# Twelve of 32 heads by the dense route, with quads ordered by three tables and dense tiles alternating between two banks

## The chip, the cores and the metric

One core of one Trainium2 chip runs the whole program. The metric is the device time in microseconds of one execution. The engines named below are PE (TensorE, matmul), PEld (its weight loads), DVE (VectorE), ACT (ScalarE), POOL (GpSimd) and SP (SyncE).

## The reference, cut to what matters

The program is a four-block tower over a stream `h` of 4 x 2048 tokens of 64 values. The change touches only the last stage, the feed-forward of block 3, which is attention whose keys and values come from a table, picked by product keys:

```python
def _pk(x, Wq_pk, pk_keys):                       # 8 heads, 64 keys a side
    q = (x @ Wq_pk).reshape(b, n, 2, 8, 32).transpose(2, 0, 1, 3, 4)
    sim = jnp.einsum('pbnhd,pkhd->pbnhk', q, pk_keys)
    scores, idx = jax.lax.top_k(sim, 16)
    index = idx[0][..., :, None] + 64 * idx[1][..., None, :]
    score = scores[0][..., :, None] + scores[1][..., None, :]
    final_scores, pk_idx = jax.lax.top_k(score.reshape(..., 256), 16)
    return softmax(final_scores), take_along_axis(index.reshape(..., 256), pk_idx)
q = (x @ Wq).reshape(b, n, 8, 64) * 64 ** -0.5
kv_scores, ind = _pk(x, Wq_pk, pk_keys)            # ind + head * 4096
k = einsum('bnhk,bnhkd->bnhd', kv_scores, keys_table[ind])
v = einsum('bnhk,bnhkd->bnhd', kv_scores, values_table[ind])
sim = einsum('bihd,bjhd->bhij', q, k)              # 2048 x 2048, causal
out = softmax(causal(sim)) @ v ; h = h + out.reshape(b, n, 512) @ Wo
```

So each (batch, head), 32 in all, needs for each token a weighted sum of 16 table rows, and then causal attention over 2048 tokens.

## The kernel before, in words

`mix_heads` does this stage. Work is cut into *quads*: 512 tokens (four tiles of 128) of one (batch, head). There are 128 quads, four to a head, and the attention tile at depth i (0 to 15) of a head looks at i+1 blocks of keys, that is at i // 4 + 1 chunks of 512.

A quad gets its mixed table rows in one of two ways. **Gathered** (6 of 8 heads of each batch, 96 quads): DVE picks the 16 rows (`top`, `top_pairs`) and turns them to row numbers (`decode`); POOL issues 16 indirect DMAs for each tile of 128 tokens, a *unit* (L2239); ACT scales each of the 16 landed rows (*copies*, `part_up`, L2430); DVE adds them up (`sum_up`, L2656). **Dense** (2 of 8 heads, 32 quads): DVE picks and ranks (`rank`, `centre`); no gather is made. Instead the whole table of the head is walked in 32 *pieces* of 128 rows. A piece is `level` (one bf16 matmul of 512 columns to the bank `DX`, L2318), `lift` (ACT, L2469), `cross` (four bf16 matmuls to the same bank, L2324 and L2325), `grow` (ACT exp, L2473) and `blend` (an f32 matmul, in two passes, that adds to `acc`, L2334). `store` (DVE, L2686) ends the quad.

All engines run through one list of *steps*, 16 to a row of 34 rows, each in its own program order. A step holds, where it exists: one attention tile n (`scores` of tile n+1 L2291, `attend` on ACT L2456, `flip` L2298, `take_flip` L2465 and `mixing` L2308 for each chunk; `peak` L2667 and `scale` L2677 on DVE), two pieces (16 steps x 2 = the 32 pieces of one dense quad), the picks of one tile of a later quad, and in three of four steps one unit of 16 copies. In every fourth step `make` turns a quad's key, value and query for attention. `scores` of tile n+1 writes the same PSUM tile `S` (four banks) that the exp of tile n reads, so it waits for that exp (`expd`); the exp of tile n+1 waits for the last mixing of tile n (`mixed`), for `peak` of tile n+1, and for whatever ACT's program has ahead of it. With one bank for pieces, `level` of a piece waits for `grow` of the one before.

POOL may run GOT = 4 units ahead of ACT's copies.

Of the kernel before, what the change touches and what calls it, by code (L numbers as in the profile page):

```python
# [13 lines left out]
ALU = mybir.AluOpType  # L14
# [1955 lines left out]
DENSE = 2  # L1970
GATHER = HEADS - DENSE
QUAD = 4
ROWS = B * DENSE * TPB // QUAD
GOT, RING = 4, 5
TILES = KEYS * KEYS // P
# [99 lines left out]
def picks(r):

    order = ("g0", "d", "g1", "g2") if r < 0 else ("d", "g0", "g1", "g2")
    return [("d", r + 1) if k == "d" else ("g", 3 * (r + 1) + int(k[1])) for k in order]


def attended(r, q):

    if r < 0 or r > ROWS:
        return None
    kind, g = (("g", 3 * r - 2), ("g", 3 * r - 1), ("d", r - 1), ("g", 3 * r))[q // QUAD]
    if g < 0 or g >= (ROWS if kind == "d" else 3 * ROWS):
        return None
    return kind, g


def mix_heads(nc, table, h, hT, ident, ones, wsim, iota, wq, wo, mask, lanes, sel, counts, push, least):

    wsim_h = wsim[:].rearrange("d (p h k) -> d h p k", p=2, h=HEADS)
    tiles = [(r, q) for r in range(0, ROWS + 1) for q in range(16) if attended(r, q)]
    number = {rq: n for n, rq in enumerate(tiles)}
    depth = [QUAD * (attended(*rq)[1] % QUAD) + rq[1] % QUAD for rq in tiles]
# [21 lines left out]
    def pieces(r, q):

        return [TILES * r + 2 * q + i for i in range(2)] if 0 <= r < ROWS else []  # L2120

    def dense_at(r):

        return 4 * [k for k, _ in picks(r)].index("d")

    def pick_before(r, q, by):

        r, q = following(r, q, -by)
        return (r, q // QUAD) if -1 <= r < ROWS - 1 else None

    def pick_after(r, q):

        r, q = following(r, q)
        return (r, q // QUAD) if q % QUAD == 0 and r < ROWS - 1 else None

    def made_at(r, q):

        ahead = number.get(following(r, q, 2))
        nxt = number.get(following(r, q))
        if q % QUAD == 2 and ahead is not None and not late(*attended(*tiles[ahead])):  # L2140
            return ahead
        if nxt is not None and nxt % QUAD == 0 and late(*attended(*tiles[nxt])):
            return nxt
        return None
# [730 lines left out]
```

## Time and profile before

| what | us |
|---|---|
| median of 3 runs | 14013.33 (14011.51 to 14019.07) |
| the profiled execution | 14017.65 |
| its span, first to last instruction | 14015.6 |
| mean granted TensorE clock over the span | 0.768 |
| busy in the span: PE, DVE, ACT, POOL | 9358.8, 9539.3, 6297.5, 7987.4 |
| first and last start of a gather (L2239) | 5841.5, 13773.4 |

Times of rows count from the start of the span. PE durations overlap (a matmul's end is modelled), so the mean of one row is longer than the pitch at which such matmuls follow each other. A row of idle time names the instruction that ended it.

### The profile page before, as it was taken

The page shows a single profiled execution, that of the slowest core. Times are in us where ns is not written, and L with a number is a line of the kernel's source. Part 1 is how long each engine was busy: PE and PEld are TensorE (multiplying, and loading weights), DVE is VectorE, ACT ScalarE, POOL GpSimd, SP SyncE. Part 2 cuts the span into 40 slices and gives each one's busy share as a digit, 9 for nine tenths or more (in the row PEclk, how much of TensorE's full clock was granted, in tenths as well). Part 3 has the DMA queues.
Part 4 walks back from the last instruction along what each step waited for, and adds up shares of the span by engine and source line. Part 5 has one row for each costly group of instructions (what it writes and reads, how often), then busy time and mean ns, then how long its engine had stood idle before and what let it go on. Part 6 is the DMA issues. An engine that isn't in the chain of part 4 may idle for free.

```text
span 14015.6 us, 129357 instructions
## 1 busy us (share of the span) xinstructions
PE 9358.8 (67%) x34236; PEld 4949.2 (35%) x34236; DVE 9539.3 (68%) x21923; ACT 6297.5 (45%) x13845; POOL 7987.4 (57%) x6892
## 2 busy tenths in 40 slices
PE   1556455455545655277887877877877877877777
PEld 0343122122213122134444434444444444444444
DVE  3332988888883874777777676677777677776751
ACT  0111333334321012156666666666666666666653
POOL 3000566666650000277777777777777777777772
PEclk9655777777775776578887888878888888888886
DMA  1000222222220000111222212212222112112220
GB/s 25 1 14 3 92 102 97 97 98 97 103 90 10 12 8 6 29 51 52 58 52 53 56 51 55 55 51 56 53 52 57 52 52 57 52 51 58 52 52 23
DMA packets 305053, 730.88 MB, mean 52 GB/s; under 512 B 130242, under 2 KB 170737, under 8 KB 269914
## 3 DMA queue, kind: packets, MB, share of 16 engines
q0 software_dynamic: 201216, 405.72, 11.1%
q1 hardware_dynamic: 103178, 317.81, 6.7%
q8 instruction: 239, 3.92, 0.1%
q14 instruction: 420, 3.44, 0.1%
HBM read 706.25 MB, written 8.42 MB: 51 GB/s over the span
## 4 chain that ended last, share of the span: by engine, by line
POOL 38%; issue 12%; PE 5%; DVE 2%; ACT 1%; DVEq 0%; DMA 0%; POOLq 0%; ACTq 0%
POOL l3m_got L2239 38%; PE l3m_O L2308 1%; PE l3m_S L2291 1%; PE l3m_T L2298 1%; PE l3m_acc L2334 1%; PE l3m_DX L2324 0%; ACT l3m_spread L2430 0%; ACT l3m_probT L2465 0%; ACT l3m_prob L2456 0%; PE l3m_T L2278 0%; DVE l3m_hot L2596 0%; DVEq L2592 0%; PE l3m_T L2265 0%; DVE l3m_hot L2593 0%; DVE l3m_hot L2589 0%
## 5 line engine op out<-in xcount | busy, mean ns | idle before, releaser
L2239 POOL DMA_INDIRECT l3m_got<-in_l_table,l3m_row x6144 | 6036.4, 982 | 1938.9 <-issue 1868.7
L2430 ACT ACTIVATE l3m_spread<-l3m_got,l3m_weight 128x128 f32<-128x128 f32 x6136 | 2109.6, 490 | 437.8 <-DMA l3m_got<-in_l_table,l3m_row 432.5
L2334 PE MATMUL l3m_acc<-l3m_W,l3m_values 128*128 128x512 f32 x2048 | 1343.8, 744 | 142.8 <-ACT l3m_W L2473 138.4
L1262 POOL TENSOR_TENSOR m_mul<-m_st,m_wide_c 128x2048 f32<-128x2048 f32 x256 | 1157.4, 4521 | 150.0 <-DVE m_st L1415 143.8
L2308 PE MATMUL l3m_O<-l3m_vo_g,l3m_probT 128*128 128x64 f32 x6528 | 1003.9, 299 | 317.7 <-ACT l3m_probT L2465 306.3
L2308 PEld LDWEIGHTS l3m_O<-l3m_vo_g,l3m_probT 128*128 128x128 f32 x6528 | 950.8, 215 | 723.7 <-ACT l3m_probT L2465 643.0
L2465 ACT ACTIVATE l3m_probT<-l3m_T 128x512 f32<-128x512 f32 (+3 forms) x1280 | 692.9, 541 | 1005.9 <-PE l3m_T L2298 1003.9
L2291 PE MATMUL l3m_S<-l3m_kvT_g,l3m_qT 64*128 64x512 f32 (+3 forms) x1920 | 751.2, 755 | 575.0 <-ACT l3m_prob L2456 561.4
L1295 PE MATMUL m_W<-m_mul,tower_ident 128*128 128x512 f32 (+1 forms) x1536 | 836.9, 667 | 206.9 <-POOL m_mul L1262 205.9
L2677 DVE SCALAR_TENSOR_TENSOR tower_h<-l3m_O,l3m_pinv,tower_h 128x64 f32<-128x64 f32 x512 | 145.4, 284 | 1195.1 <-PE l3m_O L2308 1173.6
L2469 ACT ACTIVATE l3m_V<-l3m_DX,l3k_least 128x512 bf16<-128x512 f32 x1024 | 699.5, 683 | 429.7 <-PE l3m_DX L2318 421.5
L2656 DVE TENSOR_REDUCE l3m_kv<-l3m_spread 128x128 f32<-128x2048 f32 x384 | 871.9, 2271 | 20.4 <-ACT l3m_spread L2430 20.4
L1308 PE MATMUL m_W<-m_split,l1a_sel 128*128 128x512 bf16 x1024 | 374.4, 455 | 764.6 <-DVE m_st L1415 752.7
L2298 PE MATMUL l3m_T<-tower_ident,l3m_prob 128*128 128x128 f32 x4352 | 843.1, 317 | 34.0 <-ACT l3m_prob L2456 34.0
L2473 ACT ACTIVATE l3m_W<-l3m_DX 128x512 f32<-128x512 f32 x1024 | 608.1, 594 | 409.4 <-PE l3m_DX L2325 404.6
L2298 PEld LDWEIGHTS l3m_T<-tower_ident,l3m_prob 128*128 128x128 f32 x4352 | 589.4, 172 | 452.2 <-issue 398.7
L2456 ACT ACTIVATE l3m_prob<-l3m_S,l3m_nmax 128x128 f32<-128x128 f32 (+15 forms) x512 | 589.8, 1152 | 292.8 <-DVE l3m_nmax L2667 272.7
L2667 DVE TENSOR_REDUCE l3m_nmax<-l3m_S 128x1 f32<-128x128 f32 (+15 forms) x512 | 661.2, 1291 | 40.3 <-issue 1.1
L1405 DVE TENSOR_TENSOR m_W<-m_dtx,m_W 128x1024 f32<-128x1024 f32 x512 | 618.5, 1208 | 22.0 <-PE m_W L1308 21.4
L2291 PEld LDWEIGHTS l3m_S<-l3m_kvT_g,l3m_qT 64*128 64x128 f32 x1920 | 253.5, 246 | 1032.3 <-ACT l3m_prob L2456 824.3
L1415 DVE TENSOR_TENSOR_SCAN m_st<-m_dA,m_st,m_W 128x1024 f32<-128x1024 f32 x256 | 600.8, 2347 | 22.0 <-issue 2.7
L1415 DVE TENSOR_TENSOR_SCAN m_st<-m_dA,m_W 128x1024 f32<-128x1024 f32 x256 | 585.5, 2287 | 41.3 <-POOL m_mul L1262 7.2
(677 smaller groups left out, 18538.4 us busy)
## 6 DMA issues: line engine op xcount, KB each, us to landing
m_wide_c<-l1a_c SPq DMA_DIRECT2D x256, 1024.0 KB, 4.7
l3m_got<-in_l_table,l3m_row POOLq DMA_INDIRECT x6144
l3m_values<-in_l_table SPq DMA_DIRECT2D x32, 512.0 KB, 3.9
l0i_img<-in_l_x SPq DMA_DIRECT2D x4, 1024.0 KB, 8.0
l2r_x<-l2a_hT SPq DMA_DIRECT2D x8, 512.0 KB, 5.5
qp_inw<-in_q_inw SPq DMA_DIRECT2D x1, 2336.0 KB, 7.8
l_kept<-l0t_xt,l0t_row POOLq DMA_INDIRECT x128, 2.2
l1a_c<-m_mul SPq DMA_DIRECT2D x16, 128.0 KB, 2.6
```

What stands on the lines that cost most here:

```text
L1262: pool.tensor_tensor(mul[:, k % 2], st[:, k % 2], wide_c[:, k % CRING], ALU.mult).then_inc(multiplied, 1)
L1295: last = pe.matmul(W[:, 1, lo:hi], ident[:], mul[:, k % 2, lo:hi], start=(k == 0), stop=(k == 2 * DS - 1))
L1415: dve.tensor_tensor_scan(st[:, k % 2, half(hf, k)], dA[:, k % 2, half(hf, k)], W[:, 0, half(hf, k)], first, ALU.mult, ALU.add).then_inc(sw ...
L2239: pool.indirect_dma_start(got[:, unit % GOT, j, :], None, table, bass.IndirectOffsetOnAxis(ap=row[:, unit // QUAD % RING, unit % QUAD, j:j ...
L2291: last = pe.matmul(S[:, c * CH:hi], qT[k:k + D, slot, t * P:(t + 1) * P], kvT[kind][k:k + D, c * CH:hi], start=True, stop=True)
L2298: last = pe.transpose(T[:, (a % 4) * P:(a % 4 + 1) * P], prob[:, a * P:(a + 1) * P], ident[:])
L2308: last = pe.matmul(O[:, n % 2 * D:(n % 2 + 1) * D], probT[:, (chunk0[n] + c) % 2, (a % 4) * P:(a % 4 + 1) * P], vo[kind][:, a, :], start=( ...
L2334: pe.matmul(acc[:], values[:, tile, :], W[:], start=(tile == 0), stop=(tile == TILES - 1)).then_inc(blended, 1)
L2430: last = act.activation(spread[:, unit % 2, :, j], got[:, unit % GOT, j, :], ACT.Copy, scale=weight[:, g % RING, t, j:j + 1])
L2465: act.activation(probT[:, k % 2, 0:to], T[:, 0:to], ACT.Copy).then_inc(t_taken, 1)
L2469: act.activation(V[:], DX[:], ACT.Relu, bias=least[:], scale=-1.0).then_inc(lifted, 1)
L2656: dve.tensor_reduce(out[:, ::-1, :] if g % 2 else out, spread[:, unit % 2].rearrange("p (s d) j -> p s d j", s=2), AX, ALU.add).then_inc(s ...
```

## The change

Five of the eight heads of each batch are gathered and three are dense: 20 heads (80 quads, 5120 gathers) and 12 heads (48 quads, 1536 pieces). The rows of 16 steps give way to one list of 537 steps, with three tables: the order in which quads are picked (`pick_order`), the order in which they are attended (`attend_order`), and the rates of pieces and copies. From step 9 each step has three pieces (`first_piece`), from step 13 each has ten copies (`copies`), a unit may begin and end inside a step, and tiles begin at step 24. A unit is added up by DVE in the step after its last copy.

About every second piece uses the fourth bank of `S` where neither tile n nor n+1 needs it (depth under 12, `wide`): 565 of the 1536. Where a piece and the one before it use different banks (`other`), `level` comes ahead of the earlier piece's `blend`, and waits only for the `grow` two pieces back. `scores` of a tile at depth 12 or more also waits for `grow` of the last piece that used that bank. `make` is always in the third step of a quad, and `scores` of the next tile is no longer held behind it.

```diff
-DENSE = 2
-GATHER = HEADS - DENSE
+GATHERED = (5, 5, 5, 5)
+PERIOD, BEFORE = 20, (0, 2, 4, 5, 8, 9, 10, 12, 14, 16, 18, 19)
+LAG, UNITS_FROM, PIECES_FROM = 6, 12, 9
+DQ, GQ = QUAD * len(D_HEADS), QUAD * len(G_HEADS)
+QUADS = DQ + GQ
+STEPS = QUAD * (QUADS + LAG) + 1
+COPIES = TOPK * GQ // QUADS
+def first_piece(s):
+    return TILES * DQ * (s - PIECES_FROM) // (QUAD * QUADS)
+def pick_order():
+    def due(kind, i):
+        if kind == "g":
+            return UNITS_FROM + QUAD * TOPK * i / COPIES - 6
+        return PIECES_FROM + QUAD * QUADS * i / DQ - 9
+    return sorted([("g", i) for i in range(GQ)] + [("d", i) for i in range(DQ)], key=lambda x: (due(*x), x[0]))
+def attend_order():
+    order, d = [], 0
+    for g in range(GQ):
+        if g % PERIOD in BEFORE:
+            order.append(("d", d))
+            d += 1
+        order.append(("g", g))
+    return order
...
+    second, spare = set(), False
+    for s in range(STEPS):
+        for k in pieces(s):
+            spare = not spare and not wide(s)
+            if spare:
+                second.add(k)
...
+                if i >= 3 * QUAD and behind:
+                    pe.wait_ge(grown, behind)
...
             def level(k):
                 if k % TILES == 0:
                     pe.wait_ge(taild, k // TILES + 1)
                 if k:
-                    pe.wait_ge(grown, k)
-                pe.matmul(DX[:], sel[:, k % TILES, :], ranksT[:, k // TILES % 2, :],
+                    pe.wait_ge(grown, k - 1 if other(k) else k)
+                pe.matmul(bank(k), sel[:, k % TILES, :], ranksT[:, k // TILES % 2, :],
                           start=True, stop=True).then_inc(levelled, 1)
...
             def onward(k):
+                if other(k):
+                    level(k)
                 if k >= 1:
                     blend(k - 1)
-                level(k)
+                if not other(k):
+                    level(k)
...
+                for c in range(max(chunks, len(todo))):
+                    if c < chunks:
+                        flip(n, c)
+                    if c < len(todo):
+                        cross(todo[c])
+                    if c < chunks:
+                        mixing(n, c)
+                    if c + 1 < len(todo):
+                        onward(todo[c + 1])
+                if made_at(s):
+                    make(*made_at(s))
...
+                part_up(mine[0:share])
+                chunks = depth[n] // 4 + 1 if n is not None else 0
+                for c in range(max(chunks, len(todo))):
+                    if c < chunks:
                         take_flip(n, c)
+                    if c < len(todo):
+                        grow(todo[c])
+                    part_up(mine[(c + 1) * share:(c + 2) * share])
+                    if c + 1 < len(todo):
+                        lift(todo[c + 1])
+                part_up(mine[(max(chunks, len(todo)) + 1) * share:])
```

## Rows read from the trace of the kernel before

**Rows 1.** The page: the gather, its count, busy time, mean ns, idle.
```profile
L2239 POOL DMA_INDIRECT l3m_got<-in_l_table,l3m_row x6144 | 6036.4, 982 | 1938.9 <-issue 1868.7
```
**Rows 2.** Waits from 5841 to 13773: who for whom, us in total, times, longest.
```profile
POOL l3m_got L2239 <- issue: 1868.4, 6131, 0.3
...
ACT l3m_spread L2430 <- DMA l3m_got<-in_l_table,l3m_row: 432.5, 98, 10.5
...
DVE l3m_tail L2708 <- ACT l3m_mid L2488: 163.4, 31, 10.7
...
POOL l3m_got L2239 <- DVE l3m_row L2626: 42.5, 1, 42.5
...
POOL l3m_got L2239 <- ACT l3m_spread L2430: 27.7, 11, 24.1
```
**Rows 3.** Stretches: length, busy us of PE, PEld, DVE, ACT, POOL; clock, DMA, GB/s.
```profile
8000.00:10000.00 2000.00, 1583.30 (x6542) 877.93 (x6541) 1415.77 (x4545) 1239.29 (x3111) 1526.42 (x1555) 0.82 0.21 54
13773.00:14016.00 243.00, 171.69 (x617) 115.98 (x614) 36.13 (x53) 53.55 (x87) 1.04 (x2) 0.56 0.04 10
```
**Rows 4.** The same view, eight quads: depths 0-3, 4-7, 8-11, 12-15, two of each.
```profile
8060.27:8110.11 49.84, 41.69 (x118) 18.00 (x116) 37.74 (x137) 31.61 (x89) 37.65 (x41) 0.70 0.20 53
8350.12:8408.39 58.27, 43.79 (x121) 18.86 (x119) 50.65 (x153) 32.27 (x88) 45.55 (x42) 0.69 0.18 47
8110.11:8170.54 60.43, 43.25 (x177) 22.48 (x177) 53.19 (x153) 35.82 (x93) 47.02 (x45) 0.83 0.19 49
8476.72:8535.99 59.27, 47.29 (x173) 26.55 (x171) 40.89 (x146) 35.53 (x93) 44.95 (x48) 0.80 0.20 54
8170.54:8231.08 60.54, 49.07 (x236) 29.34 (x236) 41.66 (x139) 43.04 (x106) 45.91 (x49) 0.89 0.20 52
7850.84:7916.86 66.02, 52.07 (x231) 29.25 (x232) 55.03 (x154) 39.75 (x97) 51.70 (x48) 0.82 0.21 57
7992.18:8060.27 68.09, 57.07 (x278) 35.30 (x277) 40.89 (x129) 43.31 (x102) 51.63 (x55) 0.92 0.20 53
8596.90:8665.97 69.07, 53.63 (x279) 32.57 (x278) 55.32 (x153) 43.66 (x101) 53.70 (x51) 0.88 0.18 49
```
**Rows 5.** PE by line, 5780 to 14016: busy us, mean ns, idle before.
```profile
L2334 PE MATMUL l3m_acc<-l3m_W,l3m_values 128*128 128x512 f32 x2048 | 1343.8, 744 | 142.8 <-ACT l3m_W L2473 138.4
...
L2324 PE MATMUL l3m_DX<-l3m_high,l3k_sel 128*128 128x512 bf16 x1024 | 460.1, 449 | 175.6 <-ACT l3m_V L2469 175.0
```
**Rows 6.** Timeline of PE inside one deep tile: start us, us, what.
```profile
9008.59 0.61 PE L2298 MATMUL l3m_T<-tower_ident,l3m_prob 128*128 128x128 f32 x4
9009.04 1.02 PE L2334 MATMUL l3m_acc<-l3m_W,l3m_values 128*128 128x512 f32 x2
9009.90 0.38 PE L2318 MATMUL l3m_DX<-l3m_ranksT,l3k_sel 128*128 128x512 bf16 x1
9010.13 1.11 PE L2308 MATMUL l3m_O<-l3m_vo_d,l3m_probT 128*128 128x64 f32 x8
```
**Rows 7.** Timeline of ACT, the same tile.
```profile
9015.58 1.82 ACT L2456 ACTIVATE l3m_prob<-l3m_S,l3m_nmax 128x1920 f32<-128x1920 f32 x1
...
9017.97 1.38 ACT L2430 ACTIVATE l3m_spread<-l3m_got,l3m_weight 128x128 f32<-128x128 f32 x4
```
**Rows 8.** Stretches in the head: DVE picks a gathered quad, then a dense one.
```profile
5812.33:5841.30 28.97, 4.15 (x16) 3.56 (x16) 26.05 (x116) 3.63 (x11) 0.00 (x0) 0.50 0.23 60
5841.30:5885.10 43.80, 0.33 (x2) 0.33 (x3) 38.84 (x134) 0.27 (x2) 33.83 (x33) 0.50 0.19 48
```
**Rows 9.** DVE by line, 6000 to 13700: the sum of a unit.
```profile
L2656 DVE TENSOR_REDUCE l3m_kv<-l3m_spread 128x128 f32<-128x2048 f32 x377 | 856.0, 2271 | 13.6 <-ACT l3m_spread L2430 13.6
```
**Rows 10.** First and last start of two lines: similarities, then the exp of attention.
```profile
L2257 PEld LDWEIGHTS l3m_T<-l3k_wsim,l3f_hT x1024: 182/330/336, 5809.6 to 13469.5; 64*128 64x128 f32 x171
...
L2456 ACT ACTIVATE l3m_prob<-l3m_S,l3m_nmax x512: 361/1161/1967, 6072.4 to 13982.2; 128x896 f32<-128x896 f32 x12, 128x1280 f32<-128x1280 f32 x12, 128x128 f32<-128x128 f32 x11, 128x512 f32<-128x512 f32 x11
```

More of the change, by code:

```diff
@@ L2118, in pieces @@
[L2118 to L2144, printed above, removed]
@@ new lines, in copies, with unit_summed, dense_picked, made_at @@
+    def copies(s):
+        j = COPIES * (s - UNITS_FROM - 1)
+        return range(max(j, 0), max(min(j + COPIES, QUAD * TOPK * GQ), 0))
+    def unit_summed(s):
+        ends = [j // TOPK for j in copies(s - 1) if j % TOPK == TOPK - 1]
+        return ends[0] if ends else None
+    def dense_picked(s, by):
+        p, t = pick_at(s - by)
+        return picks[p][1] if t == 0 and picks[p][0] == "d" else None
+    def made_at(s):
+        n = tile_at(s + 2)
+        return kinds[n] if n is not None and n % QUAD == 0 else None
@@ L2280, in make, with scores @@
                 last.then_inc(t_made, 1)
[L2282 to L2283 removed]
+            def scores(n, behind):
+                kind, g = kinds[n]
                 i, slot = depth[n], n // QUAD % 2
@@ L2363, in _ @@
                 if todo:
                     onward(todo[0])
-                elif r == ROWS and q == 0:
-                    blend(TILES * ROWS - 1)
-                made = made_at(r, q)
-                held = made is not None and made == nxt
-                if nxt is not None and not held:
-                    scores(nxt)
+                elif pieces(s - 1):
+                    blend(TILES * DQ - 1)
+                if nxt is not None:
+                    scores(nxt, max((k + 1 for k in second if k < first_piece(s)), default=0))
@@ L2684, in store @@
                     dve.wait_ge(placed, g)
-                dve.wait_ge(t_taken, T_at["inverse", g - 1] + 1)
+                dve.wait_ge(t_taken, T_at["inverse", g] + 1)
                 dve.tensor_tensor(stage[:], acc[:], invT[:, g % 2, :], ALU.mult).then_inc(staged, 1)
-            for r, q in steps:
-                n = number.get((r, q))
+            for s in range(STEPS):
+                n = tile_at(s)
+                todo = pieces(s)
+                done = [(i, k // TILES - 1) for i, k in enumerate(todo) if k and k % TILES == 0]
+                if not todo and pieces(s - 1):
+                    done = [(0, DQ - 1)]
+                when, held = done[0] if done else (None, None)
```

377 lines of the change are left out of this document (170 added, 207 removed).

## The prediction, made before the change was run

> **What bounds the kernel now.** I read first who never rests. POOL issues 6144 gathers in the stage, each 0.982 us long with 0.304 us of issue time behind it (1868.7 us over 6144), 1.286 us together [rows 1]. Times 6144 that is 7901 us, and the gathers run from 5841.5 to 13773.4, which is 7932 us. POOL waited for anything else for only 42.5 + 27.7 us [rows 2]. So POOL is the bound of this stage, and the first question is what stands right behind it.
>
> Next I read how late POOL's work really is to the others. The copies on ACT waited for landed rows 98 times, 432.5 us in all [rows 2]. Over 128 quads of attention that is 3.4 us a quad. This is the number on which everything hangs: the others wait for POOL for 5% of the stage, so without POOL they are at most 5% quicker by themselves.
>
> Third, the other engines in the steady stretch. In 2000 us PE is busy 1583, DVE 1416 and ACT 1239, at a granted clock of 0.82 [rows 3]. None is full. They wait for each other in turn: scores wait for the exp, the exp for mixing, mixing for ACT's copy of the flipped tile. I call that the ring. A step is 1/4 quad; POOL's bound gives 12 units x 16 x 1.291 us / 16 = 15.5 us a step (1.291 is 7932 over 6144).
>
> Fourth, what one turn of the ring costs by depth. The pairs of [rows 4] give 54.1, 59.9, 63.3 and 68.6 us a quad for one to four chunks, mean 61.5. The clock is 0.70 for the shallowest and 0.90 for the deepest quads, where PE is busy 83.8% and 77.6% of the time against 83.6% and 75.2%: PE's time in shallow quads is bought at half clock. For all 128 quads I take the first exp at 6072.4 [rows 10] to the end at 14015.6: 7943.2 us, 62.06 us a quad, which holds the tail too (243 us after the last gather, at a clock of 0.56 [rows 3]).
>
> **The change, part by part.** All terms are for one quad (four steps) unless said.
>
> *Gathers.* 1024 fewer: POOL needs 5120 x 1.291 = 6610 us, 51.6 us a quad where the ring takes over 58. It leaves the bound, and the 3.4 us go: 62.06 - 3.38 = 58.68. What is late next is the ring.
>
> *Pieces.* Three a step for two, so four more a quad. On PE at full clock a piece is a blend, 0.86 us from its start to the next matmul (9009.04 to 9009.90), and five bf16 passes at 0.23 (9009.90 to 9010.13), 2.0 us in all [rows 6]. By the mean durations of the stage it is 1.49 + 5 x 0.449 = 3.7 us [rows 5], but these overlap; scaled by 0.82, the clock of the stretch, 2.0 becomes 2.45. On ACT it adds a lift and a grow beside that. Bounds for four: 0, if they fall into time in which PE now waits (417 of 2000 us, 12.9 us a quad [rows 3]), and 4 x 2.95 = 11.8 if each is paid with its waits for `lift` (175.6 us over 1024 pieces) and `grow` (142.8 over 1024) as well [rows 5]. I split by depth. In deep quads a chunk's time on PE is all work: flip, cross, mixing, then blend and level; 4 x 2.0 is paid nearly whole, 8 us for four chunks and 7 for three. In shallow quads DVE is the longer partner: it is busy 50.65 of 58.27 us and 53.19 of 60.43 when it picks a dense quad, plus drains [rows 4]. There the third piece runs beside DVE, and the second bank takes a blend out of the way of each lift (1128 of 1535 changes of piece). I take 2 and 4 us. The mean is 5.2.
>
> *Copies.* 40 for 48 a quad. Four take 1.38 us [rows 7], one some 0.30 after another, so -2.4 on ACT. They also move: before, four copies stood last in a step, right ahead of the next exp; now that place holds one or none. But the fourth step of a quad, which had none, now has ten. Bounds -2.4 and 0; I take -1.9.
>
> *Picks and sums on DVE.* Picking a dense quad takes 43.8 us, a gathered one 29.0 plus four sums of 2.27, 38.1 [rows 8, 9]. 16 quads change sides: 16 x 5.7 = 91 us, 0.7 a quad if DVE set every step, 0 if none. There are also 16 more turns of the dense ranks (ACT's `mid`, for which DVE waited 163.4 us in 31 quads [rows 2]), up to 84 us or 0.7. I take 0.6 for both.
>
> *A wait that is new.* The scaled rows lie in two buffers, so unit u's first copy waits until unit u-2 is added up. Before, that was two steps back. Now a unit is 1.6 steps long and is added in the step after its last copy; for u = 3, 8, 13 and so on (64 of 320) the first copy falls in the same step, behind the ninth copy, in which DVE adds unit u-2 after its picks. DVE gets there some 9 to 12 us into the step (a quad's picks of 29.0 or 43.8 over four tiles, then 2.27), ACT at 7 to 12. Queued behind the waiting copy are the lift of the third piece and so PE's cross and the next exp. 64 waits of 0 to 4 us are 0 to 2.0 us a quad; I take 0.6.
>
> *Second bank, tables, held scores.* `level` ahead of `blend` is in the piece term. A deep tile's new wait for `grown` is for pieces of earlier steps, which are long done: nothing. Un-holding `scores` behind `make` (24 quads) gives under 1 us each: nothing taken. SP's table loads rise from 32 to 48 and have a head's 32 pieces of lead: hidden, as SP's loads are not among the waits.
>
> *Head and tail.* From the first similarity to the first exp it is 262.8 us [rows 10]. Now six quads are picked there, three of each kind: 3 x 43.8 + 3 x 29.0 = 218 [rows 8], with pieces from step 9 and copies from step 13 beside them. 218 to 263; I take 240, so the first exp is at 6050. At the end 16 tiles run without pieces where 12 did, all of the two deep kinds: +12 us.
>
> **The sum.** 5.2 - 1.9 + 0.6 + 0.6 = +4.5 us a quad on 58.68: 63.2. 6050 + 128 x 63.2 + 12 = 14,150. The profiled execution (14017.65, span 14015.6) is 4 us above the median of the runs, so no correction is due. Forecast: 14,150 us, +1.0%. The gain from POOL (-433 us) and the dearer ring (+576) nearly cancel, and small errors of one piece's price decide the sign: 1 us a quad is 128 us, and the break-even is at +3.4 us a quad.
>
> **The rivals.**
>
> *The clock comes back (faster).* PE works 12.26 us a step at a clock of 0.82 [rows 3], which is 10.05 us at full clock. With a third piece it is 12.05. If the denser array holds a mean clock of 0.92, as the deep quad at 7992 had it [rows 4], PE is busy 13.1 us a step, 0.8 more than now, and with the idle time that POOL does not cause (3.23 - 0.84 = 2.4) a step is 15.5; at 0.96 it is 14.95. The mean, 15.2, gives 60.8 us a quad, and with head and tail as above and 50 us for the last quads at half clock, 6050 + 7784 + 50 = 13,880. For it: the clock in [rows 4] rises with the share of work. Against it: the ring still has the exp's gap in each step (1.82 us of exp with 1.1 of PE work beside it [rows 7, 6]), and it is such gaps after which the clock is low. Chance 0.36 for this side, from -0.2% down to 13,500.
>
> The Trainium skill (TensorE: Matmul & The Clock Gate, "What's actually happening") says that the throttled clock is the default state and that activity releases it. The rows agree (0.56 in the tail, 0.92 in a deep quad); taken as strongly as it is put there it speaks for this rival.
>
> *POOL stays the bound.* If the ring had slack that the 432.5 us do not show, the gathers set the end: the first about 44 us later (a dense quad is picked first [rows 8]), 5885 + 6610 + 243 = 12,740. Against: the deepest quads already take 68 to 69 us while POOL's share is 62, so they are ring-bound now. Chance 0.03.
>
> *Each piece is paid in full (clearly slower).* With 2.95 us a piece in every step the term is 11.8 for 5.2: 14,150 + 6.6 x 128 = 14,995. The place is `cross` waiting for `lift` and `grow` waiting for `cross`, three times a step, with copies between; it decides above 0.85 us a piece (3.4 / 4). For: in a one-chunk tile there is little attention work to lay beside three pieces. Against: DVE's load hides it there. Chance of over 14,600: 0.10; it ends at the slower side like the forecast.
>
> *Nothing moves,* within 0.2% (28 us, about what a measurement of this kernel can tell from no change): the break-even by chance, 0.09.
>
> **How the numbers follow.** Forecast and its neighbourhood, 14,040 to 14,600: 0.42. Faster 0.39 (0.36 + 0.03), same 0.09, slower 0.52. With the piece term between 2 and 8.5 us the time is 13,740 to 14,570; I reach down to 13,550 for the clock and up to 14,600. The likeliest case alone: 14,040 to 14,400.
>
> **What would show it right or wrong.** Gathers with idle time between them that ends on `spread` (ACT) or on `row` (DVE), not on issue alone; the wait of `spread` for DMA gone (under 50 us) and a new one of `spread` for `kv` (DVE), some 80 us; the granted clock in the steady stretch at 0.84 to 0.88; PE busy 86 to 90% of it; quads of one chunk near 52 us, quads of four chunks near 73. A clock of 0.92 or more, or deep quads under 70 us, would make the rival right. If copies still wait for DMA by hundreds of microseconds, the first reading was wrong.

## The result, and the profile after

| what | before | after |
|---|---|---|
| median of 4 runs, us | 14012.42 (14010.05 to 14019.07) | 14271.05 (14258.20 to 14284.90) |
| profiled execution, us; its span | 14017.65; 14015.6 | 14258.20; 14256.5 |
| mean granted clock over the span | 0.768 | 0.813 |
| gathers, first and last start | 6144, 5841.5 to 13773.4 | 5120, 5887.3 to 13961.2 |
| first exp of attention [rows 10] | 6072.4 | 6058.1 |

The ratio is 1.0183, with the interval 1.0171 to 1.0196: the change costs 259 us. Forecast was +1.0%, 14,150. The sign and the range (13,550 to 14,600) held the result; the size did not come out: +138 was expected and +259 came. So two questions are left: is the first reading true (POOL is the bound, and gives 433 us back when it is relieved), and which term of the dearer ring was too small?

Shares of the whole span by the chain that ended last, from the page of after. Before, POOL had 38% of it and issue 12%, PE 5%.

```profile
PE 36%; ACT 11%; DVE 5%; issue 4%; DVEq 2%; POOL 1%; ACTq 0%; DMA 0%; POOLq 0%
```

The gather and the copy, from the page of after: count, busy us, mean ns, then idle us before them and what ended it. The first answers [rows 1].

```profile
L2258 POOL DMA_INDIRECT l3m_got<-in_l_table,l3m_row x5120 | 5065.2, 989 | 3096.4 <-issue 1516.9
L2449 ACT ACTIVATE l3m_spread<-l3m_got,l3m_weight 128x128 f32<-128x128 f32 x5120 | 1926.9, 495 | 43.0 <-issue 36.7
```

A gather costs what it cost (989 ns for 982), but 3096.4 us lie idle before them where 1938.9 did, and only 1516.9 of that is issue. What ended the rest stands in the waits of after from 5841 to 13900 (who for whom, us, times, longest), which answer [rows 2]:

```profile
POOL l3m_got L2258 <- issue: 1501.6, 4880, 1.5
...
POOL l3m_got L2258 <- ACT l3m_spread L2449: 1050.8, 165, 26.7
...
ACT l3m_W L2492 <- PE l3m_DX L2352: 678.9, 961, 2.8
...
POOL l3m_got L2258 <- DVE l3m_row L2642: 528.7, 25, 86.7
...
PE l3m_S L2312 <- ACT l3m_prob L2475: 418.6, 331, 5.0
...
DVE l3m_stage L2700 <- PE l3m_acc L2361: 300.5, 46, 14.4
...
ACT l3m_spread L2449 <- DMA l3m_got<-in_l_table,l3m_row: 6.3, 2, 5.7
```

POOL now waits for the others (1050.8 and 528.7 us), and the copies' wait for landed rows fell from 432.5 us to 6.3. No wait of `spread` for `kv` is among them.

Stretches of after, which answer [rows 3] and [rows 4]: length, busy us of PE, PEld, DVE, ACT and POOL, clock, DMA, GB/s. The third is a quad of one chunk, the fourth a quad of four, the last the tail.

```profile
8000.00:10000.00 2000.00, 1704.45 (x7258) 923.68 (x7256) 1400.27 (x4481) 1296.54 (x3051) 1226.53 (x1241) 0.90 0.17 45
...
8319.60:8382.66 63.06, 56.07 (x258) 32.38 (x257) 50.25 (x135) 42.16 (x97) 37.96 (x38) 0.89 0.17 43
8870.59:8925.15 54.56, 42.24 (x145) 17.73 (x144) 48.46 (x156) 33.44 (x89) 39.05 (x37) 0.91 0.16 44
8382.66:8461.99 79.33, 67.74 (x325) 40.65 (x324) 45.05 (x148) 50.79 (x111) 33.78 (x36) 0.89 0.15 41
14000.00:14256.00 256.00, 180.22 (x634) 123.18 (x634) 35.63 (x52) 59.41 (x102) 0.00 (x0) 0.54 0.04 9
```

(The second row is a quad of three chunks.) PE is busy 85% of the steady stretch where it was 79%, and the clock rose from 0.82 to 0.90. Over all quads of one chunk it went from 0.72 to 0.90. And still they are not shorter (54.8 us before, 55.1 after).

### The profile page after: what moved, and what is told of

It is laid out like the page before. It is cut to its first block, busy times and chain, and to the rows that moved or that the text cites. A ratio compares the mean times of both kernels' runs of the same rounds, so it can differ in the third digit from the quotient of the medians.

```text
span 14256.5 us, 136705 instructions
## 1 busy us (share of the span) xinstructions
PE 10105.4 (71%) x38012; PEld 5286.1 (37%) x38012; DVE 9606.4 (67%) x22115; ACT 6689.9 (47%) x13997; POOL 7015.6 (49%) x5868
## 4 chain that ended last, share of the span: by engine, by line
PE 36%; ACT 11%; DVE 5%; issue 4%; DVEq 2%; POOL 1%; ACTq 0%; DMA 0%; POOLq 0%
PE l3m_S L2312 7%; PE l3m_O L2329 6%; PE l3m_acc L2361 5%; PE l3m_DX L2351 5%; PE l3m_T L2319 3%; ACT l3m_spread L2449 2%; PE l3m_S L2351 2%; ACT l3m_prob L2475 2%; ACT l3m_V L2488 2%; PE l3m_T L2276 2%; PE l3m_DX L2352 1%; ACT l3m_W L2492 1%; PE l3m_T L2297 1%; POOL l3m_got L2258 1%; PE l3m_DX L2345 1%
## 5 line engine op out<-in xcount | busy, mean ns | idle before, releaser
L2258 POOL DMA_INDIRECT l3m_got<-in_l_table,l3m_row x5120 | 5065.2, 989 | 3096.4 <-issue 1516.9
L2449 ACT ACTIVATE l3m_spread<-l3m_got,l3m_weight 128x128 f32<-128x128 f32 x5120 | 1926.9, 495 | 43.0 <-issue 36.7
L2361 PE MATMUL l3m_acc<-l3m_W,l3m_values 128*128 128x512 f32 x3072 | 1791.6, 667 | 186.4 <-ACT l3m_W L2492 180.5
L2329 PEld LDWEIGHTS l3m_O<-l3m_vo_g,l3m_probT 128*128 128x128 f32 x5440 | 760.9, 206 | 251.9 <-ACT l3m_probT L2484 179.3
L2329 PE MATMUL l3m_O<-l3m_vo_g,l3m_probT 128*128 128x64 f32 x5440 | 780.5, 287 | 58.0 <-ACT l3m_probT L2484 57.9
L2312 PE MATMUL l3m_S<-l3m_kvT_g,l3m_qT 64*128 64x512 f32 (+3 forms) x1600 | 553.4, 681 | 312.3 <-ACT l3m_prob L2475 312.0
L2671 DVE TENSOR_REDUCE l3m_kv<-l3m_spread 128x128 f32<-128x2048 f32 x320 | 727.1, 2272 | 6.9 <-ACT l3m_spread L2449 6.8
L2488 ACT ACTIVATE l3m_V<-l3m_DX,l3k_least 128x512 bf16<-128x512 f32 x971 | 653.9, 673 | 159.5 <-PE l3m_DX L2345 159.2
L2361 PEld LDWEIGHTS l3m_acc<-l3m_W,l3m_values 128*128 128x128 f32 x3072 | 547.7, 204 | 449.8 <-ACT l3m_W L2492 394.0
L2312 PE MATMUL l3m_S<-l3m_kvT_d,l3m_qT 64*128 64x512 f32 (+1 forms) x960 | 532.5, 696 | 132.8 <-ACT l3m_prob L2475 132.1
```

The costliest lines, as they stand in the source:

```text
L2258: pool.indirect_dma_start(got[:, unit % GOT, j, :], None, table, bass.IndirectOffsetOnAxis(ap=row[:, unit // QUAD % RING, unit % QUAD, j:j ...
L2312: last = pe.matmul(S[:, c * CH:hi], qT[k:k + D, slot, t * P:(t + 1) * P], kvT[kind][k:k + D, c * CH:hi], start=True, stop=True)
L2329: last = pe.matmul(O[:, n % 2 * D:(n % 2 + 1) * D], probT[:, (chunk0[n] + c) % 2, (a % 4) * P:(a % 4 + 1) * P], vo[kind][:, a, :], start=( ...
L2361: pe.matmul(acc[:], values[:, tile, :], W[:], start=(tile == 0), stop=(tile == TILES - 1)).then_inc(blended, 1)
L2449: copy = act.activation(spread[:, unit % 2, :, j], got[:, unit % GOT, j, :], ACT.Copy, scale=weight[:, g % RING, t, j:j + 1])
L2488: act.activation(V[:], S[:, 3 * CH:] if k in second else DX[:], ACT.Relu, bias=least[:], scale=-1.0).then_inc(lifted, 1)
```

## The experiments

Where a kernel is compared with before or after, runs of the kernel before on the same chip stand beside it. Six kernels (`d8f`, `d8f2`, `light1`, `light4`, `warm`, `warm2`) ran on two other chips, on which the kernel before takes some 30% longer; their section says what can be read from them.

**`floor12`: before, with POOL's load cut by a quarter.** Each unit has 12 gathers in place of 16, and its copies of rows 12 to 15 read the landed rows 0 to 3 again, so that part of the mixed keys and values is another. All other work is as before.

```diff
-                for j in range(TOPK):
+                for j in range(12):
                     pool.indirect_dma_start(got[:, unit % GOT, j, :], None, table,
...
-                    last = act.activation(spread[:, unit % 2, :, j], got[:, unit % GOT, j, :], ACT.Copy,
+                    last = act.activation(spread[:, unit % 2, :, j], got[:, unit % GOT, j % 12, :], ACT.Copy,
```

> The kernel before with 12 gathers of 16 for each unit (copies 12 to 15 scale rows 0 to 3 again, so the mixed rows are not the reference's); all work of ACT, DVE and PE is kept. POOL then needs 4608 x 1.291 = 5950 us and is off the bound. My theory: the others wait for POOL only the 432.5 us of the trace, so the ring takes over at once: 13,580 us, and copies wait under 60 us for DMA. Rival: the ring had more slack than its waits show, and the time falls by 800 us or more, to 13,200 or less.

13542.92 us (13530.71 to 13557.75), ratio 0.9662 (0.9646 to 0.9678), beside 14016.32. The first two rows are waits of `floor12` from 5841 to 13900, the third its stretch.

```profile
POOL l3m_got L2239 <- ACT l3m_spread L2430: 1556.4, 221, 44.4
POOL l3m_got L2239 <- issue: 1336.6, 4386, 0.3
```
```profile
8000.00:10000.00 2000.00, 1627.31 (x6938) 897.29 (x6938) 1514.74 (x4862) 1321.50 (x3319) 1215.92 (x1237) 0.84 0.17 43
```

Relieving POOL alone gives 473 us, where the 432.5 us of the copies' waits foretold 433. From the first exp (6075.0) to the end (13540.6) it is 58.3 us a quad for 58.68, and no copy waits for a landed row any more (under 60 us was expected). The first reading stands, and so does the ring behind it.

**`d8f3`: the new list, tables, ordering and second bank, with eight dense heads as before and 12 gathers a unit.** It parts the change in two: against `floor12` it has everything but the third piece; against after it lacks the third piece with what belongs to it (16 more dense quads picked, 8 copies fewer a quad).

```diff
-GATHERED = (5, 5, 5, 5)
+GATHERED = (6, 6, 6, 6)
...
-PERIOD, BEFORE = 20, (0, 2, 4, 5, 8, 9, 10, 12, 14, 16, 18, 19)
-LAG, UNITS_FROM, PIECES_FROM = 6, 12, 9
+PERIOD, BEFORE = 12, (0, 4, 8, 10)
+LAG, UNITS_FROM, PIECES_FROM = 7, 12, 9
...
-                for j in range(TOPK):
+                for j in range(12):
...
```

> The same kernel as d8f, a third time, hoping for a chip on which the kernel before takes 14,012 us: the ring of the new list at two pieces a step. My theory: 13,400 to 13,480, so list and second bank gain 60 to 150 us and the third piece costs 790 to 870. Rival: the list costs by itself, 13,650 or more.

13617.77 us (13608.83 to 13630.70), ratio 0.9716 (0.9700 to 0.9733), beside 14013.30. It came between the two theories. The list and the bank at two pieces a step cost 75 us against `floor12` (13617.77 - 13542.92), where a gain was expected; the third piece costs the rest, 14271.05 - 13617.77 = 653 us, 5.1 us a quad. A quad of four chunks of `d8f3`, and its stretch:

```profile
8463.58:8539.24 75.66, 61.88 (x292) 38.06 (x295) 45.35 (x147) 47.77 (x110) 36.62 (x39) 0.82 0.15 41
...
8000.00:10000.00 2000.00, 1600.63 (x6690) 923.41 (x6806) 1490.03 (x4818) 1300.39 (x3280) 1206.50 (x1225) 0.83 0.16 43
```

Where it goes by depth: mean us of a quad from its first exp to the next quad's, over the 127 quads of each kernel's attention list that have a next one.

| kernel | 1 chunk | 2 | 3 | 4 | mean |
|---|---|---|---|---|---|
| before (POOL-bound) | 54.8 | 60.3 | 63.2 | 69.0 | 61.8 |
| `floor12` | 51.1 | 52.3 | 60.9 | 68.1 | 58.1 |
| `d8f3` | 48.4 | 52.7 | 58.8 | 75.5 | 58.9 |
| after | 55.1 | 56.9 | 64.0 | 80.1 | 64.0 |
| `onebank` (below) | 60.4 | 62.1 | 68.3 | 79.8 | 67.7 |

From `floor12` to `d8f3` the deepest quads lose 7.4 us, while those of one and three chunks gain 2.7 and 2.1. Where in a deep quad it is lost, the four steps of one show, in `floor12`, then in after (same columns as above):

```profile
8428.34:8445.49 17.15, 12.06 (x64) 6.57 (x63) 14.91 (x39) 12.13 (x34) 4.03 (x5) 0.95 0.06 17
8445.49:8461.55 16.06, 12.97 (x64) 7.25 (x64) 14.61 (x40) 11.20 (x26) 11.11 (x11) 0.84 0.18 45
8461.55:8477.99 16.44, 13.78 (x74) 8.68 (x75) 14.90 (x40) 11.95 (x27) 12.79 (x13) 0.90 0.17 46
8477.99:8496.62 18.63, 14.55 (x79) 9.97 (x78) 10.76 (x37) 8.48 (x14) 11.20 (x12) 0.87 0.17 44
```
```profile
8382.66:8397.93 15.27, 13.53 (x70) 7.70 (x70) 9.79 (x33) 11.68 (x32) 10.49 (x11) 1.00 0.24 67
8397.93:8416.20 18.27, 14.92 (x81) 8.64 (x79) 11.83 (x48) 12.59 (x28) 13.79 (x15) 1.00 0.21 55
8416.20:8440.52 24.32, 19.39 (x90) 12.54 (x91) 11.61 (x44) 14.73 (x32) 0.37 (x1) 0.84 0.08 25
8440.52:8461.99 21.47, 19.89 (x86) 11.78 (x84) 11.83 (x26) 11.79 (x25) 9.13 (x10) 0.78 0.11 29
```

The third step is the long one in after (24.32 us), and it is so in `d8f3` too (24.6 in the mean over deep quads, 25.7 in after, 17.3 in `floor12`), so the third piece is not its cause. Two things meet there. The queries, keys and values of the next quad are made in it (the matmuls with `wq`, by the time of their first: 8433.5 in after; in `floor12` 8489.3, in the fourth step). And in many deep quads the ranks of the next dense quad are turned just ahead of it: in 7 of 31 in `floor12`, 14 in `d8f3` and 20 in after. PE around the third step of another deep quad of after, a dense one (start us, us, what, and in brackets the idle time ahead of it):

```profile
8627.57 0.61 PE L2377 MATMUL l3m_T<-tower_ident,l3m_ranks 128*128 128x128 f32 x4
8628.86 0.66 PE L2377 MATMUL l3m_T<-tower_ident,l3m_centred 128*128 128x128 f32 x4 [0.69 <-ACT l3m_ranksT L2496]
8629.36 1.02 PE L2361 MATMUL l3m_acc<-l3m_W,l3m_values 128*128 128x512 f32 x2
8630.22 0.38 PE L2345 MATMUL l3m_DX<-l3m_ranksT,l3k_sel 128*128 128x512 bf16 x1
8633.04 6.04 PE L2312 MATMUL l3m_S<-l3m_kvT_d,l3m_qT 64*128 64x512 f32 x8 [2.44 <-ACT l3m_prob L2475]
...
8651.77 1.12 PE L2284 MATMUL l3m_T<-l3f_hT,l3k_wq 64*128 64x512 f32 x2
8653.67 0.63 PE L2290 MATMUL l3m_T<-tower_ident,l3m_kv 128*128 128x128 f32 x4 [0.78 <-ACT l3m_qT L2457]
8654.98 1.96 PE L2297 MATMUL l3m_T<-l3k_wo,l3m_kvT_g 64*128 64x64 f32 x8 [0.69 <-ACT l3m_kvT_g L2460]
8657.42 2.07 PE L2276 MATMUL l3m_T<-l3k_wsim,l3f_hT 64*128 64x128 f32 x8 [0.47 <-ACT l3m_vo_g L2465]
```

And ACT at the first of these:

```profile
8629.56 0.60 ACT L2500 ACTIVATE l3m_shown<-l3m_T 128x512 f32<-128x512 f32 x1 [0.75 <-PE l3m_T L2377]
8630.51 0.63 ACT L2502 ACTIVATE l3m_high<-l3m_shown 128x512 bf16<-128x512 f32 x1 [0.36 <-issue]
8631.05 1.84 ACT L2475 ACTIVATE l3m_prob<-l3m_S,l3m_nmax 128x1920 f32<-128x1920 f32 x1
```

`make` is a serial chain between PE and ACT. With the similarities that follow it (L2276) it takes 7.7 us, from 8651.77 to 8659.5, with 1.94 us of idle PE in three waits (0.78 + 0.69 + 0.47). The exp (1.84 us, from 8631.05) stands behind ACT's two turning operations (`shown` and `high`), so PE has 2.44 us of nothing. Then the eight score matmuls take 6.04 us at a mean granted clock of 0.60; in the second step of the same quad, after a gap of 1.32 us, eight of them took 3.48 (8612.84) at 1.00.

Over the deep quads, steps three and four together went from 36.4 us (17.3 + 19.1) in `floor12` to 41.8 (24.6 + 17.2) in `d8f3`: 5.4 us a deep quad, 170 us over 32. Split by what happens in a deep quad (one quad of each kernel fits none of the groups), the mean us of steps three and four are:

| kernel, deep quads | `make` in step | ranks turned | quads | steps 3 + 4 |
|---|---|---|---|---|
| `floor12`, gathered | 4 | no | 16 | 34.2 |
| `floor12`, dense | 4 | no | 7 | 35.6 |
| `floor12`, gathered | 3 | yes | 7 | 41.3 |
| `d8f3`, gathered | 3 | no | 16 | 38.3 |
| `d8f3`, gathered | 3 | yes | 7 | 44.3 |
| `d8f3`, dense | 3 | yes | 7 | 46.4 |

So the place of `make` goes with some 4 us, and the turning with 6 more, and the new list turns ranks in a deep quad twice as often as the old one. It is the deep dense quads that lose most: they take 88.9 us in `d8f3` for 69.9 in `floor12`, the gathered ones 70.9 for 67.6. A second thing shows in the same quads. PE's work in a deep quad is the same in both kernels (busy time by clock, 49.6 us in `floor12` and 49.7 in `d8f3`), but the granted clock fell from 0.88 to 0.81, which makes 56.1 busy us into 61.5; idle time of PE rose by 2.1 us only. That the lower clock follows from the new place of `make` and of the turning may be, but no run moved either of them alone, so it is not shown.

**`onebank`: after, with all dense tiles in their own bank.** Only the second bank of the change is undone.

```diff
-            spare = not spare and not wide(s)
+            spare = False
```

> The changed kernel with no piece in the second bank (every piece in DX, level behind blend as before). If the second bank hides a blend of 0.86 us in shallow quads and DVE does not cover it: 1128 changes of piece x up to 0.86 = up to +970 us; I expect a quarter of it, since DVE sets the shallow steps: +150 to +300, so 14,420 to 14,570. Rival: DVE covers all of it, within 60 us of the changed kernel.

14738.83 us (14724.08 to 14758.84), ratio 1.0514 (1.0497 to 1.0532): 468 us above after, where 150 to 300 was expected. Waits of `onebank`, 5841 to 13900:

```profile
ACT l3m_W L2492 <- PE l3m_DX L2352: 1072.7, 1397, 2.0
PEld l3m_DX L2351 <- ACT l3m_V L2488: 985.6, 969, 4.1
...
ACT l3m_V L2488 <- PE l3m_DX L2345: 618.4, 1100, 2.7
```

`level`, `lift`, `cross` and `grow` of one bank are a chain between PE and ACT; a second bank lets one piece's `level` run while ACT still does the `grow` of the piece before. By the table it is worth 5.3, 5.2 and 4.3 us in quads of one to three chunks and nothing in the deepest, in which it is not used. So DVE does not cover shallow quads: if it set their length, as I had argued, a longer chain on PE and ACT would have been hidden.

**`d8` and `d10`: how many heads.** `d8` has the whole change but eight dense heads, `d10` ten. The attention lists are these; in both, the first quad of a gathered head is made while the last tiles of the head before still read that buffer, so some tiles read the next head's keys and values; the work is the same.

```diff
+GATHERED = (6, 6, 6, 6)
+PERIOD, BEFORE = 3, (2,)
...
+GATHERED = (6, 5, 6, 5)
+PERIOD, BEFORE = 11, (1, 3, 6, 8, 10)
```

> The changed kernel with eight dense heads as before (six of eight gathered, 12 copies and two pieces a step, a dense quad attended after every third gathered one): the tables and the second bank alone. POOL issues 6144 gathers again, 7932 us. If POOL's bound holds, the time is 13,980 to 14,050, whatever the second bank brings. Rival: the list of steps itself is worse (a fourth step with copies, no held scores), and costs over 100 us: 14,120 or more.

> The changed kernel with ten dense heads (6, 5, 6, 5 gathered; 11 copies a step and 2.5 pieces on average). POOL 5632 x 1.291 = 7271 us, 14.2 us a step. My theory, with the ring at 58.7 us a quad at 8 dense and 65.1 at 12 as measured: 61.9 a quad less 0.4 of tail, 6055 + 128 x 61.9 = 13,980 by a straight line; since shallow quads hide their pieces and deep ones pay them, 13,850 to 14,020. Rival: what costs at 12 is a threshold (the third piece in a step of four chunks), then 10 is near the ring of 8, 13,650 to 13,800.

`d8`: 14051.51, ratio 1.0024 (1.0014 to 1.0033). Its gathers run from 5890.4 to 13806.6, the pitch of before (7916 us over 6144 for 7932), only some 49 us later at the start, and its copies wait 400.0 us for landed rows. The time lies 1.5 us above the range that was expected, and the rival (14,120 or more) is out. With 6144 gathers POOL hides everything that the list costs or brings.

`d10`: 14094.96, ratio 1.0052 (1.0035 to 1.0069), above both ends of what was expected of it. POOL's waits for ACT (504.2 us) and for DVE (277.1) say that it is off the bound already, so the ring's price comes in.

**`d9`: nine dense heads.** A list worked out for it (period 92, 36 dense quads, lag 7, 11.5 copies a step) and else as after.

```diff
+GATHERED = (6, 6, 6, 5)
...
+PERIOD, BEFORE = 92, (0, 4, 7, 8, 12, 15, 16, 20, 23, 24, 28, 30, 32, 36, 38, 40, 43, 44, 48, 51, 52, 56, 59, 60, 64, 66, 68, 71, 72, 76, 79, 80, 84, 87, 88, 91)
+LAG, UNITS_FROM, PIECES_FROM = 7, 12, 9
...
+COPIES = TOPK * GQ / QUADS
...
+        j, e = int(COPIES * max(s - UNITS_FROM - 1, 0)), int(COPIES * max(s - UNITS_FROM, 0))
+        return range(j, max(min(e, QUAD * TOPK * GQ), j))
...
```

> The changed kernel with nine dense heads (6, 6, 6, 5 gathered), 11.5 copies and 2.25 pieces a step, a lag of seven quads, and a dense quad placed ahead of the first gathered quad of each head and 13 others. All of the reference is computed. POOL: 5888 gathers x 1.291 = 7601 us, 59.4 a quad, first gather at 5887, so not under 13,740. The ring: 13,543 at two pieces a step (the old list with POOL off the bound) and some 14,050 to 14,100 at 2.5. My theory, the two bounds cross between 8 and 10 dense heads: 13,780 to 13,900, faster than both kernels. Rival: an uneven number of pieces in a step costs by itself (2 in one, 3 in the next), and the time is 13,950 or more.

13967.75 us over 8 runs (13952.38 to 13997.22), ratio 0.9968 (0.9957 to 0.9978): 45 us faster than before, and the fastest kernel here that computes the whole. It missed the upper end of the expected time by 68 us and lies in the range of the rival (13,950 or more). Waits, 5841 to 13900:

```profile
DVE l3m_stage L2700 <- PE l3m_acc L2361: 274.9, 34, 24.7
...
POOL l3m_got L2258 <- ACT l3m_spread L2449: 208.2, 42, 14.2
...
ACT l3m_spread L2449 <- DMA l3m_got<-in_l_table,l3m_row: 94.7, 19, 10.6
```

Both POOL and the ring wait a little for each other (208.2 and 94.7 us): here the two bounds cross. The crossing has a price: a straight line by pieces a step between `d8f3` and after gives an estimate of 13,781 us for nine heads (2.25) and 13,944 for ten (2.5), and the gathers alone, 256 fewer than in `d8` at 1.291 us, one of 13,721 for nine. Measured were 13,968 and 14,095, 187 and 151 above the higher of these. DVE waits for the last blend of a dense quad 274.9 us, once 24.7, for 96.1 and 4.6 at most in `d8f3`; but after, with three pieces in every step, has 300.5 and 14.4. So whether the uneven list costs, as the rival says, is open.

**On two other chips: `d8f`, `d8f2`, `light1`, `light4`, `warm`, `warm2`.** `d8f` and `d8f2` are the kernel of `d8f3`, `warm2` is that of `warm`. The `light` kernels leave out two of the three `cross` passes (the weights' lower bits are dropped), for tiles of depth 12 and more (`light4`) or under 4 (`light1`). `warm` adds four matmuls of 256 columns ahead of the wait for the exp.

```diff
-                for i, x in enumerate((high, mid, tail)):
+                for i, x in enumerate((high,) if k in lit else (high, mid, tail)):
```
```diff
+                if n >= 2:
+                    pe.wait_ge(scaled, n - 1)
+                for _ in range(4):
+                    pe.matmul(O[:, 2 * D:6 * D], push[:], sel[:, 0:2, :].rearrange("p a b -> p (a b)"),
+                              start=True, stop=True)
```

> The changed kernel with eight dense heads, a lag of seven quads, a dense quad attended before gathered quads 0, 4, 8 and 10 of every 12, and 12 gathers of 16 for each unit (copies 12 to 15 scale rows 0 to 3 again, so the mixed rows are not the reference's). POOL is off the bound, so this is the ring of the new list at two pieces a step; beside the 13,543 us of the old list without POOL's bound it gives what list and second bank are worth, and what is left up to 14,271 us is the price of the third piece. My theory: list and bank gain some 60 to 150 us at two pieces, 13,400 to 13,480, and the third piece costs 6 to 7 us a quad (790 to 870 us). Rival: the list itself costs, 13,650 or more, and the third piece is under 5 us a quad.

> The changed kernel without the mid and tail matmuls of a piece (two of five bf16 passes, 0.43 us at full clock) in steps whose tile has four chunks; the dense weights lose their low bits there. 384 pieces x 0.43 = 165 us at full clock, 184 at a clock of 0.90. My theory: PE sets the deep steps, so all of it comes back, -150 to -200 us. Rival: ACT's chain sets them, under 80 us.

> The same two matmuls left out in steps whose tile has one chunk, also 384 pieces. My theory: DVE's picks set most of the shallow steps, so a third or less comes back, 0 to -60 us. Rival: PE sets these too (or the ring of lift, cross and grow, in which the two passes stand), and -150 us or more come back.

> The changed kernel with four bf16 matmuls of 256 columns on constants, to columns of the bank of O that nobody reads, ahead of each wait for the exp (and a wait for scale of the tile before, so that the bank is free). They fill 0.44 us of PE's 1.3 us gap at full clock. If the half-rate stretches follow that gap, the granted clock rises from 0.90 to 0.94 or more in the steady stretch and the time falls by 100 to 350 us. If they follow the longer gaps (make, the dense ranks), the clock stays within 0.01 and the time is the same or up to 100 us longer.

> The same kernel as d8f, again, because in the call that ran it every engine stood still for microseconds at a time with nothing to wait for, and the kernel before took 18,544 us there: the changed kernel with eight dense heads and 12 gathers of 16 a unit, the ring of the new list at two pieces a step. My theory: 13,400 to 13,480 us on a chip that runs the kernel before in 14,012. Rival: the list itself costs, 13,650 or more.

> The same kernel as warm, again for the same reason: four bf16 matmuls of 256 columns on constants ahead of each wait for the exp. If the half-rate stretches follow that gap, the granted clock of the steady stretch rises from 0.90 to 0.94 or more and the time falls by 100 to 350 us from 14,271; if not, it stays within 0.01 and the time is the same or up to 100 us longer.

| kernel | us | before on that chip | ratio |
|---|---|---|---|
| `d8f` | 16370.59 | 18543.62 | 0.8826 (0.8811 to 0.8841) |
| `light4` | 17897.69 | 18543.62 | 0.9641 (0.9619 to 0.9663) |
| `light1` | 17885.69 | 18543.62 | 0.9651 (0.9635 to 0.9667) |
| `warm` | 17977.34 | 18543.62 | 0.9694 (0.9677 to 0.9712) |
| `d8f2` | 16102.71 | 18358.47 | 0.8769 (0.8754 to 0.8785) |
| `warm2` | 17750.35 | 18358.47 | 0.9661 (0.9644 to 0.9679) |

The ratios to before say nothing of the chip of the result, since before gains and loses there by something else (last section). After itself did not run there, so none of the gains that were expected of `light4`, `light1`, `warm` and `warm2` can be read. What stands is the comparison between kernels of one chip. `light4` and `light1` are 12 us apart, with 81 us between `light4`'s own runs: leaving out two passes brings the same in deep and in shallow quads, whatever that is. The forecast had split the piece's price 8 to 2 between them. `warm` is 92 us above `light1`, and the clock in its stretch of 8000 to 10000 is 0.77 for 0.76. Whether columns that only keep PE busy would pay on the chip of the result was not tried and is open.

## Why the prediction was right, and where it was short

The balance, all in us of the medians: 14,012 before; -470 by POOL off the bound (forecast -433); +75 by list, tables and bank at two pieces a step; +653 by the third piece with its picks and fewer copies; 14,270, and 14,271 was measured. It adds up by construction, since the three differences are between neighbours; each kernel between is a measured one. Against the forecast, the relief brought 37 us more, the third piece cost 154 us more, and list, tables and bank cost what had been set down for a wait that did not come: together 115 of the 121 us that were missed.

**POOL's relief** was right in mechanism and size. The sum of the waits that others had for the bound, 432.5 us, was all but some 40 us of what a lighter POOL brought, though POOL then waited 1556.4 us for ACT. The rival in which POOL stays the bound is out.

**The third piece** was the mis-sized term. Forecast: 5.2 for pieces, -1.9 for copies, 0.6 for picks, 3.9 us a quad; measured 5.1, which is 154 us more. What a piece costs PE at full clock was right. PE in a deep tile of after, from one blend to the next mixing:

```profile
8618.56 1.10 PE L2361 MATMUL l3m_acc<-l3m_W,l3m_values 128*128 128x512 f32 x2
8619.49 0.38 PE L2345 MATMUL l3m_DX<-l3m_ranksT,l3k_sel 128*128 128x512 bf16 x1
8619.71 0.60 PE L2319 MATMUL l3m_T<-tower_ident,l3m_prob 128*128 128x128 f32 x4
8620.65 0.39 PE L2351 MATMUL l3m_DX<-l3m_high,l3k_sel 128*128 128x512 bf16 x1 [0.34 <-ACT l3m_V L2488]
...
8621.52 1.00 PE L2329 MATMUL l3m_O<-l3m_vo_d,l3m_probT 128*128 128x64 f32 x8
```

The blend and level are 1.15 us (8618.56 to 8619.71), the other four passes 0.87 (8620.65 to 8621.52): 2.02 for the forecast 2.0. The split by depth failed. I had 2, 4, 7 and 8 us a quad, which less 1.9 for copies is 0, 2, 5 and 6; the table gives 6.7, 4.2, 5.2 and 4.6 (after less `d8f3`). The premise "There the third piece runs beside DVE" is what fell: `onebank` shows that in quads of one chunk the chain of the pieces itself sets the length. DVE's high busy share there (50.65 of 58.27 [rows 4]) was read as a limit, and was none.

One term was put at nothing without a reason: 16 more quads are not only picked but also attended by the dense route, and their scores cost PE more. Two deep gathered tiles of after, both at a granted clock of 1.00, stand against a dense one, of the quad shown above:

```profile
8612.84 3.48 PE L2312 MATMUL l3m_S<-l3m_kvT_d,l3m_qT 64*128 64x512 f32 x8 [1.32 <-ACT l3m_prob L2475]
...
8796.79 1.98 PE L2312 MATMUL l3m_S<-l3m_kvT_g,l3m_qT 64*128 64x512 f32 x8 [0.69 <-ACT l3m_prob L2475]
8812.15 1.98 PE L2312 MATMUL l3m_S<-l3m_kvT_g,l3m_qT 64*128 64x512 f32 x8 [1.32 <-ACT l3m_prob L2475]
```

Over all of after the scores of a tile take 2.8 us in the mean for a dense quad and 1.7 for a gathered one; over the 64 tiles that change sides that is some 65 us of the 154, as an estimate, if all of it is paid. In the kernel the keys of a gathered head alternate between two halves of the rows from chunk to chunk, those of a dense head all lie in one (`key_rows`); that this is the reason no run shows.

**List and make.** "Un-holding `scores` behind `make` (24 quads) gives under 1 us each: nothing taken" is the step that failed here. The scores no longer wait behind `make`, but in 23 deep quads `make` went from the fourth step into the third, in many beside the turning of ranks, and steps three and four of a deep quad take 5.4 us more. Quads of one and three chunks gave most of that back, and 75 us remained, 0.6 a quad. By luck the term for the new wait (0.6 a quad) was as large; that wait is not there. `spread` waits for `kv` nowhere in after, and in `d8`, `d8f3`, `d9` and `d10` for 18.6 to 28.9 us only. ACT comes to the first copy of a unit after DVE has added up its buffer, not before, as I had timed it.

**The rest of the sum:** first exp 6050 forecast, 6058.1 measured. From there to the end it is 8198.4 us, 64.05 a quad for 63.2: 109 us of the miss. With the 8 us of the head, and without the 12 us that I had added for the end (64.05 holds the tail), it is 105; the other 16 are rounding and the profiled execution, which was 13 us under the median. One bound was added up wrongly: 2.45 with 0.17 and 0.14 of waits is 2.76 us a piece and not 2.95, so a quad's bound is 11.0 and the rival that pays it in full stands at some 14,890. No other number used it.

**The rival of the clock** came halfway, and its own terms tell why it lost. By steps (span from the first exp over 512; PE's busy and idle time in 8000 to 10000 over the steps in it; busy time by the clock):

| kernel | step | PE busy | idle | busy x clock |
|---|---|---|---|---|
| before | 15.51 | 12.28 | 3.23 | 10.07 |
| `floor12` | 14.58 | 11.86 | 2.72 | 9.96 |
| `d8f3` | 14.73 | 11.79 | 2.94 | 9.78 |
| after | 16.01 | 13.65 | 2.37 | 12.28 |
| `onebank` | 16.91 | 13.88 | 3.03 | 12.49 |

Its idle time (2.4) came out at 2.37, its work (12.05) at 12.28. The clock was 0.90 where it took 0.92 to 0.96: 12.05 over 0.94 is 12.8, and 13.65 came. From `d8f3` to after PE's work rose by 2.5 us a step at full clock. Its busy time rose by 1.86 only, since the clock rose from 0.83 to 0.90; 0.57 of that fell into time in which PE had been idle (up to 0.2 of it may be matmul records missing from the trace of `d8f3`, 6690 for 6806 weight loads), and 1.28 us a step, 5.1 a quad, were paid. The Trainium skill (TensorE: Matmul & The Clock Gate, "What's actually happening") has the throttled clock as the default and activity as what releases it; the trace agrees in direction, 0.82 to 0.90 with PE's share from 79% to 85%, and 0.54 in the tail, but a fuller array did not bring full clock here.

**The signs asked for:** gathers that wait for ACT and DVE, yes (1050.8, 528.7); `spread` for DMA under 50, yes (6.3); `spread` for `kv`, some 80, no (none); clock 0.84 to 0.88, it was 0.90; PE busy 86 to 90%, it was 85.2; one chunk near 52, it was 55.1; four near 73, it was 80.1. Deep quads over 73 and a clock over 0.88 pull to different sides, and the first won.

## What to carry to other kernels

When one engine is always busy, add up how long the others wait for its results: here that sum (432.5 us), not its own load, came near to what relieving it brought (473). Set against it the work that the relief puts on the ring behind it, for each turn and by the depth of the turn, and where a serial chain such as `make` moves, price the place where it lands, beside its length. Between "bound by the helper" and "bound by the ring" lies a count at which both wait a little; here it was nine heads, and of the kernels that compute the whole only it beat the kernel before, by 0.3%.

A high busy share of an engine is not its being the limit: lengthen the other chain (`onebank`), and see if the time stands still.

## What the runs showed of the hardware that was not expected

On two other chips the same kernel before takes 18543.62 and 18358.47 us. The gathers of `light1` are as long there as those of after (947 ns in the median for 944), and ACT's copies too (494 ns in the mean for 495), but engines stand still for some microseconds with nothing to wait for that the profile shows. PE in a quad of `light1` there:

```profile
8052.66 0.38 PE L2345 MATMUL l3m_DX<-l3m_ranksT,l3k_sel 128*128 128x512 bf16 x1
8056.20 2.08 PE L2363 MATMUL l3m_acc<-l3m_W,l3m_values 128*128 128x512 f32 x2 [3.16 <-issue]
8065.80 0.61 PE L2353 MATMUL l3m_DX<-l3m_high,l3k_sel 128*128 128x512 bf16 x1 [7.52 <-ACT l3m_V L2490]
```

What does it the profile does not show. There `d8f` gains 12% over before where the same kernel gained 2.8% on the chip of the result, so ratios were not carried from one chip to the other.

Eight score matmuls took 3.48 us and 6.04 us in neighbouring steps of one quad, at a granted clock of 1.00 and 0.60.

The clock does not go by PE's busy share alone, and the forecast, with half clock as a trait of shallow quads, did not have that. Over all quads of one chunk, and over those of four, the granted clock and in brackets the busy share of PE are:

| kernel | one chunk | four chunks |
|---|---|---|
| before | 0.72 (77%) | 0.88 (82%) |
| `floor12` | 0.76 (79%) | 0.88 (82%) |
| `d8f3` | 0.82 (74%) | 0.81 (81%) |
| after | 0.90 (80%) | 0.87 (85%) |
| `onebank` | 0.90 (74%) | 0.88 (85%) |

From `floor12` to `d8f3`, with the new list and the second bank, it rose in quads of one chunk and fell in those of four; with one more piece a step it is 0.90 and 0.87.
